# Row sums of a causal attention kernel: a chunk's first tile goes into the ring, and GpSimd takes two more key tiles of a quad

## What is computed

```python
scores = jnp.einsum('bthd,bshd->bhts', q, k)
mask = jnp.tril(jnp.ones((T, T), dtype=scores.dtype))
scores = scores * mask
attn = jax.nn.softmax(scores / T ** 0.5, axis=-1)
out = jnp.einsum('bhts,bshd->bthd', attn, v).reshape(B, T, H * Dh)
...
g = _silu(_L0_ffn_ref(xn, ...))
x = x + s * g
```

## Time and profile before

| what | value |
|---|---|
| runs | 1534.5 us (1533.64 to 1537.15) |
| profiled execution | 1533.04 us, its span 1531.3 us |
| busy | PE 1484.9 (97%), DVE 1045.5 (68%), POOL 865.7 (57%), ACT 773.8 us (51%) |
| adds, line 885 | 308, 598.9 us; idle before them 150.8 us, 128.0 of it until line 1444 |
| row sums, line 1450 | 1072 instructions (two for a matmul), 124.8 us |
| exponentials, line 1015, into Pb | 1122, 518.4 us |
| VectorE's maxima, line 1132 | 768, 484.5 us |
| TensorE's granted clock, span | 0.993 |

### The profile page before, as it was taken

The page is one execution under the profiler, slowest core; times in us unless marked ns, Lnnn a source line. Parts: engine busy times, 40 slices in busy tenths (PEclk is TensorE's granted clock), DMA queues, the critical chain, the costliest instruction groups (busy, mean ns, idle before and its releaser), DMA issues. The chain is left out here.

```text
span 1531.3 us, 24566 instructions
## 1 busy us (share of the span) xinstructions
PE 1484.9 (97%) x8554; PEld 899.1 (59%) x8554; DVE 1045.5 (68%) x2413; ACT 773.8 (51%) x1614; POOL 865.7 (57%) x723
## 2 busy tenths in 40 slices
PE   5999999999999999999999999999999999999898
PEld 4788888888544455555554545545455554543586
DVE  7546666544787777777777777777777777773367
ACT  4333322332545656656566566656666666667211
POOL 4100000000566878778887787877878778777501
PEclk9999999999899999999999999999999999999999
DMA  6568965548824514242450542424155161124588
GB/s 208 180 183 233 262 188 164 165 142 216 227 49 113 123 39 104 85 105 53 116 118 23 140 110 50 106 86 105 42 124 113 30 139 51 51 83 138 187 300 307
DMA packets 118348, 201.26 MB, mean 131 GB/s; under 512 B 23216, under 2 KB 40752, under 8 KB 117200
## 3 DMA queue, kind: packets, MB, share of 16 engines
q1 hardware_dynamic: 118224, 199.69, 47.5%
HBM read 123.02 MB, written 76.09 MB: 130 GB/s over the span
## 5 line engine op out<-in xcount | busy, mean ns | idle before, releaser
L885 POOL TENSOR_TENSOR acc<-acc,Pb 128x1024 f32<-128x1024 f32 (+2 forms) x308 | 598.9, 1974 | 150.8 <-PE psO L1444 128.0
L1015 ACT ACTIVATE Pb<-psS 128x512 f32<-128x512 f32 (+2 forms) x1122 | 518.4, 532 | 302.0 <-PE psS L1421 291.7
L1132 DVE TENSOR_REDUCE mx<-psM 128x1 f32<-128x512 f32 x768 | 484.5, 683 | 148.8 <-PE psM L1321 147.6
L1421 PE MATMUL psS<-half 97*128 97x512 f32 (+1 forms) x1247 | 475.0, 398 | 12.3 <-ACT Pb L1015 8.9
L1321 PE MATMUL psM<-half 96*128 96x512 f32 (+3 forms) x1280 | 457.6, 383 | 8.0 <-DVE mx L1129 3.1
L1421 PEld LDWEIGHTS psS<-half 97*128 97x128 f32 x1247 | 234.3, 190 | 252.3 <-issue 104.9
L1321 PEld LDWEIGHTS psM<-half 96*128 96x128 f32 x1280 | 235.3, 190 | 79.3 <-DVE mx L1132 28.7
L1129 DVE CUSTOM_DVE_ANT_0 psM<-psM,negm 128x256 f32<-128x256 f32 (+3 forms) x512 | 238.3, 518 | 56.7 <-PE psM L1321 56.1
L1444 PE MATMUL psO<-Pb,Vs 128*32 128x512 f32 (+3 forms) x2304 | 266.9, 534 | 2.2 <-POOL Pb L868 2.2
L1149 DVE TENSOR_TENSOR st_lo<-psP,st_hi 128x512 fp32r<-128x512 f32 x64 | 43.9, 688 | 118.7 <-ACT st_hi L977 118.7
L1450 PE MATMUL psL<-Pb,ones 128*32 128x512 f32 (+3 forms) x1072 | 124.8, 535 | 0.0
(11 more groups left out here) (103 smaller groups left out, 1478.2 us busy)
## 6 DMA issues: line engine op xcount, KB each, us to landing
half<-q_hi SPq DMA_DIRECT2D x32, 512.0 KB, 9.8
half<-k_hi SPq DMA_DIRECT2D x32, 512.0 KB, 9.7
xt<-in_L_attn_x SPq DMA_DIRECT2D x8, 1024.0 KB, 8.2
q_hi<-st_hi SPq DMA_DIRECT2D x32, 256.0 KB, 4.5
q_lo<-st_lo SPq DMA_DIRECT2D x32, 256.0 KB, 4.8
gate<-gs SPq DMA_DIRECT2D x32, 256.0 KB, 2.2
k_hi<-st_hi SPq DMA_DIRECT2D x32, 256.0 KB, 2.8
k_lo<-st_lo SPq DMA_DIRECT2D x32, 256.0 KB, 2.9
```

What stands on the lines that cost most here:

```text
L885: g.tensor_tensor(to[:, :, o:], to[:, :, o:], Pb[s % RING][:, heads, o:], ALU.add).then_inc(sum_done, 1)
L1015: a.activation(weights(s, h)[:, o:], score_bank(s * HQ + h, last)[:, o:], ACT.Exp, scale=SCALE).then_inc(exp_done, 1)
L1132: ins = v.tensor_reduce(flat[:, heads, slots], bank[:, 0:ns * w].rearrange("p (a b c) -> p a b c", a=nh, c=w), AX.X, ALU.max)
L1421: t.matmul(score_bank(n, last)[:, o:], Ks[par][j // HALF][0:MROW + 1, h, j % HALF * P:(j % HALF + 1) * P], Qs[par][c // 2][0:MROW + 1, h, ...
```

## The change

The first tile of chunks 1 to 3 now goes into the ring as every other does; only step 0 of a quad still goes into acc. Its GpSimd add is then of two ring tiles, acc = Pb[tile 0] + Pb[tile 1], and waits for an earlier use of acc (L_full, two chunks back) instead of the value product. ScalarE's waits for the ring follow: a place that holds a first tile is free when the add of the tile behind it is done. Beside this, who sums a tile is now decided tile by tile: in quads 0 to 6 GpSimd adds (2,2) and (3,2) as well, and in the last quad it no longer adds (3,7) and (3,11). Where the first tile for TensorE's row sums is (c,4), the wait for psL stands there.

```diff
+EXTRA = [(2, 2), (3, 2)]
+def by_gpsimd(s, last):
+    c, j = STEPS[s]
+    if last and c > 0 and (on_diagonal(s) or (c, j) in [(3, 7), (3, 11)]):
+        return False
+    return j % 2 == 1 or not last and (c, j) in EXTRA
+def by_tensor(s, last):
+    return STEPS[s][1] > 0 and not by_gpsimd(s, last)
+def added_with(s):
+    c, j = STEPS[s]
+    return s + 1 if c > 0 and j == 0 else s
...
-            return Pb[s % RING][:, h, :] if j else acc[c % 2][h // 2][:, h % 2, :]
+            return Pb[s % RING][:, h, :] if s else acc[0][h // 2][:, h % 2, :]
...
-                    if j == 0:
+                    fresh = c > 0 and j == 1
+                    if fresh:
+                        pool.wait_ge(L_full, START + qn * NCH + c - 1)
+                    elif j == 1:
                         pool.wait_ge(pv_done, START + qn * NSTEP + s)
...
-                        g.tensor_tensor(to[:, :, o:], to[:, :, o:], Pb[s % RING][:, heads, o:], ALU.add).then_inc(sum_done, 1)
+                        one = Pb[(s - 1) % RING][:, heads] if fresh else to[:, :, o:]
+                        g.tensor_tensor(to[:, :, o:], one, Pb[s % RING][:, heads, o:], ALU.add).then_inc(sum_done, 1)
...
-                if j == 0:
-                    act.wait_ge(L_full, START + qn * NCH + c - 1)
+                if s == 0:
+                    act.wait_ge(L_full, START + qn * NCH - 1)
                 else:
                     act.wait_ge(pv_done, START + qn * NSTEP + s - RING + 1)
-                    if s % 2:
-                        act.wait_ge(sum_done, START + (qn * NG + summed_before(max(0, s // 2 - 1), last) - (s < 2)) * NPAIR)
+                    if s > RING:
+                        taken = added_with(s - RING)
+                        if by_gpsimd(taken, last):
+                            act.wait_ge(sum_done, START + (qn * NADD + added_before(taken + 1, last)) * NPAIR)
...
-                    if j > 0 and j % 2 == 0 or not summed(s // 2, not more):
-                        if j == 2:
+                    if by_tensor(s, not more):
+                        first = not any(by_tensor(i, not more) for i in range(s - j, s))
+                        if first:
                             pe.wait_ge(lst_done, START + qn * NCH + c)
```

More of the change, by code:

```diff
@@ L95, in diagonals_before, with added_before @@
     return sum(on_diagonal(i) for i in range(s))
[L98 to L105, removed]
+EXTRA = [(2, 2), (3, 2)]
[6 more added lines that the diff above has]
+    return STEPS[s][1] > 0 and not by_gpsimd(s, last)
+def added_before(s, last):
+    return sum(by_gpsimd(i, last) for i in range(s))
+NADD = added_before(NSTEP, False)
+def added_with(s):
+    c, j = STEPS[s]
+    return s + 1 if c > 0 and j == 0 else s
 OWN_STEPS = 19
@@ L529, in weights @@
         def weights(s, h):
-            c, j = STEPS[s]
-            return Pb[s % RING][:, h, :] if j else acc[c % 2][h // 2][:, h % 2, :]
+            return Pb[s % RING][:, h, :] if s else acc[0][h // 2][:, h % 2, :]
         def tail(body):
@@ L866, in select, with add @@
                         pool.wait_ge(exp_done, START + exps + s * HQ + 2 * p + 2).then_inc(pool_waited, 1)
-                        tile = (Pb[s % RING][:, 2 * p:2 * p + 2] if j else acc[c % 2][p])[:, :, o:o + P]
+                        tile = (Pb[s % RING][:, 2 * p:2 * p + 2] if s else acc[0][p])[:, :, o:o + P]
                         g.affine_select(out=tile, in_=tile, compare_op=ALU.is_ge, fill=0.0, base=0,
                                         pattern=[[0, 2], [1, P]], channel_multiplier=-1).then_inc(sel_done, 1)
[L871 to L874, removed]
-                    if j == 0:
+                def add(s):
+                    c, j = STEPS[s]
+                    o = max(0, j - CT * c) * P
+                    fresh = c > 0 and j == 1
+                    if fresh:
+                        pool.wait_ge(L_full, START + qn * NCH + c - 1)
+                    elif j == 1:
                         pool.wait_ge(pv_done, START + qn * NSTEP + s)
@@ L882, in add @@
                             pool.wait_ge(exp_done, START + exps + s * HQ + 2 * p + 2)
-                        if j > 0:
-                            pool.wait_ge(sum_done, START + (qn * NG + summed_before(gr, not more)) * NPAIR + p - 1)
-                        g.tensor_tensor(to[:, :, o:], to[:, :, o:], Pb[s % RING][:, heads, o:], ALU.add).then_inc(sum_done, 1)
+                        if j > 1:
+                            pool.wait_ge(sum_done, START + (qn * NADD + added_before(s, not more)) * NPAIR + p - 1)
+                        one = Pb[(s - 1) % RING][:, heads] if fresh else to[:, :, o:]
+                        g.tensor_tensor(to[:, :, o:], one, Pb[s % RING][:, heads, o:], ALU.add).then_inc(sum_done, 1)
                 def later_keys(qn, c):
@@ L910, in quad @@
                         select(s + 1)
-                        if j > CT * c and summed(gr, not more):
-                            add(gr - 1)
-                            add(gr)
-                    else:
-                        add(gr)
+                        if j > CT * c and by_gpsimd(s + 1, not more):
+                            add(s - 1)
+                            add(s + 1)
+                    else:
+                        for tile in (s, s + 1):
+                            if by_gpsimd(tile, not more):
+                                add(tile)
                     for masked in masked_keys(qn, gr):
@@ L1004, in exps @@
                 o = max(0, j - CT * c) * P
-                if j == 0:
-                    act.wait_ge(L_full, START + qn * NCH + c - 1)
+                if s == 0:
+                    act.wait_ge(L_full, START + qn * NCH - 1)
                 else:
                     act.wait_ge(pv_done, START + qn * NSTEP + s - RING + 1)
-                    if s % 2:
-                        act.wait_ge(sum_done, START + (qn * NG + summed_before(max(0, s // 2 - 1), last) - (s < 2)) * NPAIR)
+                    if s > RING:
+                        taken = added_with(s - RING)
+                        if by_gpsimd(taken, last):
+                            act.wait_ge(sum_done, START + (qn * NADD + added_before(taken + 1, last)) * NPAIR)
+                    elif s < RING and qn > 0 and by_gpsimd(NSTEP + s - RING, False):
+                        act.wait_ge(sum_done, START + ((qn - 1) * NADD + added_before(NSTEP + s - RING + 1, False)) * NPAIR)
                 for h in range(HQ):
@@ L1450, in values @@
                             ins = t.matmul(psL[h * DH:(h + 1) * DH, o:], ones[:, 0:DH], weights(s, h)[:, o:],
-                                           start=(j == 2), stop=False, skip_group_check=True)
+                                           start=first, stop=False, skip_group_check=True)
                     ins.then_inc(pv_done, 1)
                 def row_sums(qn, c, final):
-                    last = FIRST[c + 1] if c + 1 < NCH else NG
-                    pe.wait_ge(sum_done, START + (qn * NG + summed_before(last, final)) * NPAIR)
+                    last = STEPS.index((c + 1, 0)) if c + 1 < NCH else NSTEP
+                    pe.wait_ge(sum_done, START + (qn * NADD + added_before(last, final)) * NPAIR)
                     for h in range(HQ):
```

## The result

The changed kernel takes 1515.1 us (median of 4 runs, 1512.9 to 1518.7), the kernel before 1535.8 in the same comparison: ratio 0.987, 95% interval 0.984 to 0.990. Forecast were 1518.5 us, with 1511 to 1526 as the range. The profiled execution took 1513.03 us with a span of 1511.3, 20.0 us less than before.

What follows compares the result with a forecast made beforehand. TensorE was taken to bound the seven full quads and GpSimd's chain the last one. Gains of 7.5 and 8.0 us took 15.5 off the profiled 1533.04, giving 1517.5; the forecast was put 1 above, 1518.5 us, range 1511 to 1526.

Steps and rivals of the forecast that it cites:

- Full quads, 7.5 us forecast: Seven full quads: two row-sum steps fewer on TensorE save 12.1 us, less 4.6 lost to VectorE's wait in chunk 3.
- I cost these waits at nothing: Full quads: new ring waits of exponentials on GpSimd's sums or earlier value products were claimed to cost 0.
- The row sums themselves: Full quads: each row-sum step off TensorE worth 0.86 us; in chunk 3, 0.66 of it lost behind VectorE.
- 4.5 us of cover before the divide: Chunk 3, full quad: GpSimd's adds end at 765.8, its DMA-bound divide starts at 770.32, so later work stays put.
- Last quad, 8.0 forecast: Last quad: GpSimd's chain in chunk 3 stops ending steps; 8.0 us gained, taken between workings of 7.3 and 9.5.
- The working link by link: Last quad, chunk 3: with TensorE the only limit from 1401 on, its end moves from 1436.1 to 1426.6, 9.5 us.
- the sum of idle time and clock: Last quad: 7.25 us of TensorE idle plus 1.8 of clock, less 1.7 for added row sums, gives 7.3 us.
- the first (VectorE's wait costs nothing): Full quads give all 12.1 us and the last quad 9.5: 1512.5 us, chance 0.17.
- The second (GpSimd late in the full quads): GpSimd's late adds and selects cancel the full quads' gain, only the last quad gains: 1526 us, chance 0.15.
- The third (the last quad gives only 3 us): ScalarE or the output stage's loads end the last quad, 3 us gained instead of 8: 1523.5 us, chance 0.08.
- the fifth (nothing measurable): Whole kernel: gains eaten by waits not found, 1533 to 1536 us, chance 0.02.
- The fourth (dearer adds): Full quads: GpSimd's adds 0.5 us dearer each without rest, 27 us lost in seven: 1545.5 us, chance 0.04.

Runs made afterwards that it cites:

- ring only: Changed kernel with only the first tile in the ring and its two-tile add; who sums which tile as before the change: 1527.8 us, ratio 0.992 to 0.996.
- later reciprocal: Changed kernel with VectorE's third reciprocal of a quad, and its DMA wait, ahead of the maxima of step (3,4) instead of (3,3): 1508.3 us.
- (3,4) for (3,2): Changed kernel with GpSimd adding (3,4) instead of (3,2) in quads 0 to 6, VectorE's reciprocal left ahead of step (3,3): 1510.7 us.
- without the ring: Changed kernel with the first tile of each chunk kept in acc as before, the new division of tiles between GpSimd and TensorE kept: 1527.3 us.
- four tiles: Changed kernel with GpSimd adding (2,2), (2,4), (3,2) and (3,4) in a full quad instead of two tiles: 1533.5 us, ratio 0.997 to 1.000.
- the last quad's tiles back: Changed kernel with (3,7) and (3,11) of the last quad given back to GpSimd: 1521.0 us, ratio 0.988 to 0.991.
- (2,2) in the last quad: Changed kernel with VectorE's third reciprocal ahead of step (3,4) and GpSimd adding (2,2) in the last quad too: 1508.3 us.

## Why the prediction was right, and what it missed

The mechanism was right: GpSimd's waits for the value product were the room for two tiles, TensorE bound the full quads and GpSimd the last one, and VectorE's DMA wait took most of the second row sums. Two terms of the sum were too small: the forecast for the profiled execution was 15.5 us, and it gained 20.0.

1. Full quads, 7.5 us forecast for seven, which is 6.4 for six; 10.6 measured in quads 1 to 6. By chunk the six gave 4.1 us in chunk 1, where nothing was forecast, 4.9 in chunk 2 (5.2 forecast) and 1.4 in chunk 3 (1.2 forecast). Quad 0 gained nothing, with the lower clock in its chunk 2. The step that failed is "I cost these waits at nothing". It looked only at waits that the ring adds, and not at one that it takes away: the exponentials of (2,1) waited for the sum of (1,5), since GpSimd had begun chunk 1 late. The row stood in the earlier trace rows, 705.19 with 0.50 us for GpSimd, and I used it only for its start. It is worth 0.6 us in each quad; ring only shows it alone. Two quads before (55.2 and 55.5 us in chunk 3) and one after (55.3) were longer than the rest; why, these runs do not show.
2. The row sums themselves: 0.86 us forecast for chunk 2, 0.8 measured. Chunk 3: 0.2 forecast, usually 0.1 measured, TensorE's gap 0.54 against 0.6. The later reciprocal and (3,4) for (3,2) both give back 0.8, so the cause is shown. One detail was wrong: VectorE's wait for the DMA did not grow, it is 1.31 us in both, and from its row-sum addition to the reciprocal it takes 4.40 us in both (the earlier trace rows and the rows above). In another I had luck: I had left GpSimd 4.5 us of cover before the divide, and 2.71 were there. The adds ended where I had put them, 16.0 us behind the last mark, but the divide's DMA was there 1.8 us sooner after it. Before the change this wait was 2.8 to 4.9 us in quads 0 to 6, and the quad that I had read has the longest. A cover read in one quad was too large, and it did not matter for two tiles; for the third of 4.7 us it does.
3. Last quad, 8.0 forecast, 9.4 measured. The working link by link gave 9.5 and would have been right; I took a middle because the sum of idle time and clock gave 7.3. That sum missed that ScalarE's late exponentials also stretched the steps around the gaps. TensorE's rows at one of them, before and, below, at the same place after (psM is a bank for scores here):

```profile
1402.97 0.50 PE L1421 MATMUL psM<-half 97*128 97x512 f32 x1
...
1404.37 0.99 PE L1421 MATMUL psS<-half 97*128 97x512 f32 x2 [0.67 <-ACT Pb L1015]
1405.29 1.07 PE L1444 MATMUL psO<-Pb,Vs 128*32 128x512 f32 x8
```

```profile
1392.91 0.51 PE L1451 MATMUL psM<-half 97*128 97x512 f32 x1
1393.25 0.87 PE L1451 MATMUL psS<-half 97*128 97x512 f32 x3
1394.05 1.06 PE L1474 MATMUL psO<-Pb,Vs 128*32 128x512 f32 x8
```

The gap is 0.67 us, but the way from the first row to the last is 2.32 us against 1.14. Laid side by side through chunk 3, the instructions that both kernels have took 11.1 us longer before: 6.5 in gaps, 1.9 in the last products at the lower clock, and 2.7 in such steps. Two row sums more take back 1.8, which leaves about 9.4. So the idle time and the clock were near what the sum had, and the steps were missing from it.
4. GpSimd's load, 113 us forecast, is 113.4; the adds are 332, the row sums 976; the output stage moved with the attention.

Of the rivals, the first (VectorE's wait costs nothing) is out: chunk 3 gave 0.1 us and not 0.86. The times alone would not have told it from the forecast, since 1515.1 lies between its 1512.5 and my 1518.5, and the period of 126.6 is its 126.5. It came there by chunk 1's 0.6 us, that I had missed, and not by chunk 3; of its two figures the 9.5 for the last quad was the better one. The second (GpSimd late in the full quads) is out for this change but is what happens without the ring and with four tiles. The third (the last quad gives only 3 us) and the fifth (nothing measurable) are out by the 9.4 and the ratio. The fourth (dearer adds) is out: the adds of the full quads took 4.7 us a pair, beside 5.6 and 5.7 in places of the last quad, where VectorE splits weights and inputs. The Trainium skill, "GPSIMD Engine Reference", section 4.1, keeps two-input elementwise work off GpSimd. Here two tiles on it paid and four did not: the idle time decided. No run here has these adds on VectorE, so none tests the rule's comparison of the two.

## What to carry to other kernels

An engine's busy share did not say here how much more it could take; the length of its waits just ahead of the next thing that others need from it did (2.7 us took no further tile of 4.7). Read that length in several periods. Before moving work there, look for a wait that an in-place operation makes, and let it write elsewhere. When work is taken off the bounding engine, look which engine stands at a DMA just behind that place: the same work a few steps on, or the wait one step later, was worth 0.8 us here instead of 0.1.

## What was unexpected of the hardware

TensorE's granted clock fell in quad 0 in some executions and at different places, and no gap in its timeline was longer than 0.35 us in the chunk where it fell. Chunk 1 took 33.5 us at 1.00 in the changed kernel and 35.7 at 0.86 with the later reciprocal; chunk 2 took 47.8 at 0.96 and 46.1 at 1.00. What decides it these runs do not show. It moved these chunks by about 2 us each, which stands beside a spread between runs of 5.8 us (1512.9 to 1518.7).

A lower clock did not always cost time. In four other executions (the last quad's tiles back, no ring, (3,4) for (3,2), and (2,2) in the last quad) chunk 1 of quad 0 had a clock of 0.95 and took the same 33.5 us. At full clock TensorE waits for a DMA near the end of that chunk:

```profile
436.70 0.50 PE L1451 MATMUL psS<-half 97*128 97x512 f32 x1 [0.97 <-DMA half<-mrow]
```

In the six executions with 0.95 or 0.86 in that chunk this wait is gone: the slower stretch had used it up.
